# Expert stages: bf16 products that nobody reads, placed where PE waits

## What is computed

```
# L1 (stages moe1_first, moe1_second): gated experts
probs = softmax(x @ gate_w.T);  w, idx = top_k(probs, 2);  w = w / sum(w)
for each expert e of 8:
    g, u = split(x @ gate_up_proj[e].T)           # 512 + 512 columns
    out += combine[:, e] * ((silu(g) * u) @ down_proj[e].T)

# L2 (stages moe2_first, moe2_second): experts and one shared expert
shared = silu(x @ shared_w1.T) @ shared_w2.T
gates  = softmax(top_k(x @ gate_w.T, 2)) at the chosen experts
out    = shared + sum_e gates[:, e] * (silu(x @ experts_w1[e].T) @ experts_w2[e].T)
```

## Time and profile before

| | us |
|---|---|
| median of 3 runs | 4015.75 |
| lowest, highest | 4010.53, 4017.01 |
| profiled execution, its own time | 4004.72 |
| its span | 4002.9 |

### The profile page before, as it was taken

One profiled execution on the slowest core, in us unless ns is written; L12 is line 12 of the kernel. 1 busy time (PEld: TensorE's weight loads), 2 busy tenths in 40 slices (PEclk: granted clock), 3 DMA queues, 4 the chain that ended last, 5 costly groups with the idle time before them and its releaser, 6 DMA issues. The chain is left out here.

```text
span 4002.9 us, 60331 instructions
## 1 busy us (share of the span) xinstructions
PE 3291.2 (82%) x19635; PEld 1996.3 (50%) x19635; DVE 2708.6 (68%) x7212; ACT 1828.9 (46%) x2668; POOL 1013.6 (25%) x1089
## 2 busy tenths in 40 slices
PE   4659999977576967999999869789767996997898
PEld 2422333344355852222222258668656774886687
DVE  8888888576776458999999564464566445544453
ACT  1225666665122531677777725323222333553454
POOL 3442430021334631000000036426501571000000
PEclk8869999998787976999999969889877998998899
DMA  1042331000021122000000031221201112000100
GB/s 48 1 140 76 113 113 38 2 1 1 22 86 46 47 72 88 19 18 19 26 19 11 22 147 47 75 88 45 83 1 70 36 52 102 0 0 1 53 0 21
DMA packets 88138, 185.24 MB, mean 46 GB/s; under 512 B 24560, under 2 KB 43056, under 8 KB 84784
## 3 DMA queue, kind: packets, MB, share of 16 engines
q1 hardware_dynamic: 60704, 116.03, 8.7%
q0 software_dynamic: 26576, 64.79, 5.4%
q10 hardware_dynamic: 576, 0.79, 0.1%
HBM read 119.92 MB, written 60.82 MB: 45 GB/s over the span
## 5 line engine op out<-in xcount | busy, mean ns | idle before, releaser
L2125 ACT ACTIVATE core_pr<-core_two 128x1024 f32<-128x1024 f32 (+3 forms) x896 | 794.3, 933 | 440.0 <-PE core_two L2087 439.2
L2151 DVE TENSOR_REDUCE core_mx<-core_one 128x1 f32<-128x512 f32 x1280 | 800.6, 682 | 21.6 <-PE core_one L2071 18.1
L2071 PE MATMUL core_one<-arena,core_q_sb 64*128 64x512 bf16 (+3 forms) x1792 | 548.8, 381 | 106.7 <-DMA core_q_sb<-core_q_sb 44.5
L2071 PEld LDWEIGHTS core_one<-arena,core_q_sb 64*128 64x128 bf16 x1792 | 140.7, 94 | 690.1 <-DVE core_mx L2151 525.5
L2098 PE MATMUL core_ps_o<-core_pr,core_vals 128*32 128x512 f32 (+3 forms) x3584 | 438.1, 561 | 1.6 <-ACT core_oT L2129 0.5
L2087 PE MATMUL core_two<-core_q_sb,arena 64*128 64x512 bf16 (+3 forms) x1792 | 362.2, 361 | 6.4 <-ACT core_pr L2125 5.4
L2148 DVE CUSTOM_DVE_ANT_0 core_junk<-core_one,behind 128x128 bf16<-128x128 f32 (+3 forms) x512 | 230.3, 486 | 59.3 <-PE core_one L2071 53.9
L2019 POOL COPY core_vals<-arena 128x288 f32<-128x288 f32 x32 | 14.5, 455 | 979.2 <-PE core_ps_o L2098 979.2
L340 POOL DMA_INDIRECT expert_out<-arena,moe_first_dest_index x142 | 139.9, 985 | 100.6 <-ACT arena L512 89.9
L340 POOL DMA_INDIRECT expert_out<-arena,moe_second_dest_index x142 | 139.9, 985 | 99.7 <-ACT arena L512 90.0
L336 POOL DMA_INDIRECT arena<-expert_rows,moe_first_row_index x142 | 137.4, 968 | 98.6 <-DVE moe_first_dest_index L614 55.9
(11 more groups left out here) (532 smaller groups left out, 7350.4 us busy)
## 6 DMA issues: line engine op xcount, KB each, us to landing
arena<-expert_out SPq DMA_DIRECT2D x64, 256.0 KB, 3.1
core_q_sb<-q_parts SPq DMA_DIRECT2D x384, 32.0 KB
arena<-k_parts SPq DMA_DIRECT2D x360, 32.0 KB
expert_rows<-arena SPq DMA_DIRECT2D x16, 512.0 KB, 11.6
core_w_raw<-in_m_up POOLq DMA_DIRECT2D x25, 256.0 KB, 4.0
m_hi<-core_w_hi POOLq DMA_DIRECT2D x25, 256.0 KB, 2.8
m_lo<-core_w_lo POOLq DMA_DIRECT2D x25, 256.0 KB, 3.3
q_parts<-qkv_parts SPq DMA_DIRECT2D x16, 384.0 KB, 2.6
```

The source lines that it names most:

```text
L2071: pe.matmul(one[bank][:, 0:width], q_sb[rows, hq, pair, qt * P:(qt + 1) * P], k_sb[rows, hq, pair, kc * CW:kc * CW + width], start=True, s ...
L2125: a.activation(pr[:, k % 2, hp, :, off:CW], two[hp][:, :, off:CW], ACT.Exp, scale=HD ** -0.5).then_inc(s_exp, 1)
L2151: v.tensor_reduce(mx[:, h * TPB + qt, kc:kc + 1], one[bank][:, 0:width], AX.X, ALU.max).then_inc(s_read, 1)
```

## The change

A function `warm(n)` issues n products of 128 x 128 (the table of ones, stationary) by 128 x 512 (the other table, its 128 columns read four times) in bf16 into `bank[7]`. Nobody reads them, they wait for nothing and signal nothing. PE issues 12 at the stage's start, behind the wait for the stage's weights; 3 after the logits of each chunk but the last, except where a unit of the shared expert stands (so after chunks 0 to 6 in a gated stage, after 0, 1, 3 and 5 in a shared one); and 11 behind the last table product and, in a shared stage, the last `all_down` before the slots. Nothing is removed, and the other engines' queues are as before.

```diff
--- before.py
+++ after.py
@@ -390,8 +390,13 @@
                     if i == UNITS - 1:
                         all_down(i)
 
+            def warm(n):
+                for _ in range(n):
+                    pe.matmul(bank[7][:], r.ones[:], r.beforeb[:].unsqueeze(1).to_broadcast([P, 4, P]), start=True, stop=True)
+
             for sem, n in loaded:
                 pe.wait_ge(sem, n)
+            warm(12)
             turn(0)
             for c in range(CHUNKS):
                 if c + 1 < CHUNKS:
@@ -399,6 +404,8 @@
                 logits(c)
                 if c in EARLY:
                     always(1)
+                elif c + 1 < CHUNKS:
+                    warm(3)
             always(CHOOSING)
             pe.wait_ge(s_chain, TOTAL)
             pe.matmul(ps_p[:, 0:E], r.beforeb[:], tot[:], start=True, stop=True)
@@ -414,6 +421,7 @@
                     always(ASIDE)
             if shared:
                 all_down(BEFORE - 1)
+            warm(11)
 
             def turn_x(s):
                 pe.wait_ge(s_row[s % R], rows0[s % R] + 16 * (s // R + 1))
```

## The result

The changed kernel takes 4022.3 us (median of 10 runs, 4017.33 to 4032.47) against 4009.99 us (10 runs, 4002.24 to 4017.01): a ratio of 1.0028, 95% interval 1.002 to 1.0037. That is 8 to 15 us slower; the prediction had +10.5 (4026 us, range 4004 to 4038).

A forecast was written before the change was run, and what follows sets the result against it. In an expert stage's opening PE's own speed, at granted clock 0.50, was taken to set the time. Gated threes +16.0, shared threes -2.0 and the eleven -3.5 made +10.5 on 4015.75: 4026 us, range 4004 to 4038.

The forecast's parts named there:

- The gated threes: Three products between chunks in both gated stages: run at clock 0.50, logits 8.0 us later a stage, +16.0 us together.
- the hole behind the twelve: Gated stages' start: twelve products end after 2.8 us, PE idles 2.7 or 3.4 us, and the clock falls; cost 0.
- The row at 3082.5: Profile row before the change: PE idled 2.52 us after full work and the clock fell; taken as model for the hole.
- Rival 1: Clock holds through the gated chunks: -3.7 us a gated stage, -23.5 us in all, 3992 us; chance 0.14.
- The shared threes: Three products after chunks 0, 1, 3 and 5 of both shared stages: -2.0 us together, bounds -8.9 to +10.2.
- held: Shared chunk phases with the clock at 1.00 after the twelve's lift: 19.0 us each, -8.9 us for both stages.
- falls: Shared chunk phases where the clock falls and returns with the units: products cost up to 5.1 us a stage, +10.2 together.
- The eleven: Eleven products before the first gathered row, four stages: fit PE's 4.7 us wait without delay, and gain 3.5 us together.
- The bound of -10.8: Largest gain of the eleven in four slot openings, 2.7 us at most each; the other bound was 0.
- The sum: Whole kernel: +16.0 - 2.0 - 3.5 = +10.5 us, 4026 us on the median, 0.26% slower; chance 0.60.

The follow-up runs named there:

- experiment 1: The kernel before plus only three products between chunks in the two gated stages; 4028.04 us against 4011.65, ratio 1.0037.
- experiment 8: The changed kernel with 24 products in place of 12 ahead of the gated stages' first transposes, threes kept; ratio 0.9998 to the kernel before.
- experiment 9: The changed kernel with 4 products in place of 3 between gated chunks, the twelve kept; ratio 1.0013 to the kernel before.
- experiment 4: The changed kernel with, in gated stages, 24 first products in place of 12 and 4 between chunks in place of 3; 4002.26 us against 4011.65, ratio 0.9973.
- experiment 5: The kernel before plus only 24 products ahead of the first transposes and 4 between chunks in gated stages; 4006.58 us against 4011.79, ratio 0.9986.
- experiment 6: The kernel of experiment 4 with, in shared stages, 16 first products in place of 12 and 4 in place of 3; 3997.15 us against 4011.79, ratio 0.9964.
- experiment 10: The kernel of experiment 6 plus 3 and 2 products behind the first two gathered rows' transposes; 3989.6 us against 4011.79, ratio 0.9947.
- experiment 12: The kernel of experiment 6 without the eleven products before the first gathered row, on slower chips; 4106.3 us against 4117.58, ratio 0.9968.
- experiment 3: The kernel before plus only the 11 products ahead of the first gathered row, all four stages; 4010.61 us against 4011.65, ratio 1.0002.
- experiment 11: The kernel before plus the 11 products and 3 and 2 behind the first two gathered rows' transposes, on slower chips; ratio 0.9992.
- experiment 2: The changed kernel without the three products between chunks in the two gated stages; 4012.46 us against 4011.65, ratio 0.9997.

## Why the prediction came out

**The gated threes.** Forecast +16.0 by a clock that falls with the hole behind the twelve and doesn't come back; +15.0 in the trace, +15 us by the threes alone (experiment 1). The missing 1 us lies in the products' price: they lengthened a chunk's period from 2.47 to 3.65 us, by 1.18 and not by 1.28, seven times a stage. The row at 3082.5 was the right one to go by: the hole, 2.83 us in both stages where 2.7 and 3.4 were forecast, was not survived, though by the rule of the Trainium skill (TensorE: Matmul & The Clock Gate, "Why this matters for your kernels"), which allows idle gaps up to about 3 us, it would have been. The measurement decides: the clock fell at 1185.0, 1.3 us after PE had resumed.

The reason was right, but narrower than the truth. I put the fall down to the hole and expected a filled hole to cure it. Experiment 8 filled it, and with three a chunk kept the clock in one stage of two; experiment 9 left it, and with four the clock came back. Only the two together, 24 and 4, kept it through every gated phase profiled (ten, in experiments 4, 5, 6, 10 and 12). Rival 1's price (17.0 us a phase) was met by the phase of experiment 8 that held (17.10), and with more products by experiment 4.

**The shared threes.** Forecast -2.0. The trace has -4.8, and that is chance: over five traces with and six without, the phases are on average 1.7 us longer with them, a difference within their scatter. What was mis-sized is the weighing between "held" (-8.9) and "falls" (+10.2): I went below the middle, towards "held", and only two phases of ten held. I credited the units with keeping the clock; where it fell, it fell 1.4 to 5.6 us after the first transposes, before the first unit.

**The eleven.** Forecast -3.5; -4.1 in the trace, -4.5 in that of the eleven alone. That they delay nothing was right: the first gathered row's transpose follows the table products after 4.75 us, before 4.73. The bound of -10.8 was too wide: with the clock at 1.00 in all four openings they were 8.3 us shorter (experiment 10). In the traces the gain is still there at the last slot (experiment 3); whether it reaches the end in full stays open, since the medians of experiments 3, 11 and 12 do not agree on it.

**The sum.** +15.0, +1.7 and -4.1 make +12.6, against 12.3 by the medians. That these agree to 0.3 us is luck, as the 1.7 is uncertain by about its own size. The forecast of 10.5 was near because its largest term was right in mechanism and size; the two small ones, -2.0 and -3.5, can be wrong by several us without leaving its range. The 4026 us lie above the measured 4022.3 although the change was put too low, because they start from 4015.75, the median of three runs of the kernel before; over ten runs it is 4009.99.

## What to carry to other kernels

Products that nobody reads are free only in two ways: in a wait that they do not outlast at the clock of that moment, or by keeping a clock that would fall. Count them for both clocks: twelve fill 5.1 us at 0.50 and 2.8 us at 1.00, and a burst sized for the first leaves a hole at the second. On a path where the engine is the bound, put in enough that the clock stands in every profile taken, or none: 3 a chunk cost 7.5 us a stage, none cost nothing, 4 with a full first burst gained 2.8.

## What the runs showed of the hardware

- Two gated phases with the same code gave 17.10 and 27.95 us in one execution (experiment 8), and moe2_first's phase took 19.48 to 28.26 us with the same products in five kernels; without products it went from 21.30 to 28.99 us. In such a stretch where the clock turns is a matter of chance, and one profile says little about it.
- At a granted clock of 0.50, three 512-column products between gated chunks (one chunk every 3.65 us) did not bring it back in 28 us, in four phases of two kernels (the changed one and experiment 1); four (one chunk every 4.08 us) brought it back after 13.7 and 10.3 us (experiment 9).
- With three products a chunk the clock fell during a wait of 1.1 us in some phases (ahead of 2608.89 in experiment 2, of 2332.24 in experiment 8) and stood through the same wait in others (ahead of 2626.23 in the changed kernel, and in the other gated phase of experiment 8). With four, and 24 or 16 ahead, the same wait, 0.90 us then, was survived in all sixteen phases of experiments 4, 5, 6, 10 and 12.
- From the fifth gathered row to the last, a gated stage took 187.2 us in all ten traces of the faster chips, at whatever clock its opening ran, and 209.0 to 209.6 us in the four of the slower ones.
